# Eight-head layers: two rows half a trip apart, attention steps of one between feed-forward products of the other

## The reference

```python
def _layer(x, wqkv, qs, ksc, wo, lg, lb, w1, b1, w2, b2):
    h = shift_token(x)                 # second half of the features comes from the token before
    q, k, v = split(h @ wqkv)          # 8 heads of 64
    q = l2norm(q) * qs;  k = l2norm(k) * ksc
    q, k = rotary_xpos(q, k)
    o = local_attention(q, k, v)       # 4 windows of 128, each sees itself and the one before
    x = x + o @ wo
    h = layernorm(shift_token(x)) * lg + lb
    a, g = split(h @ w1 + b1)          # 682 columns each
    return x + (a * gelu(g)) @ w2 + b2
```

## Time and profile before

| | us |
|---|---|
| median of three runs | 2756.39 |
| profiled execution | 2757.84 |
| its span, first to last instruction | 2756.1 |
| first row transpose of the layers | 1282.3 |
| share of the layers | 1473.8 |

### The profile page before, as it was taken

One profiled execution on the slowest core, in us unless ns is written; L12 is line 12 of the kernel. 1 busy time (PEld: TensorE's weight loads), 2 busy tenths in 40 slices (PEclk: granted clock), 3 DMA queues, 4 the chain that ended last, 5 costly groups with the idle time before them and its releaser, 6 DMA issues.

```text
span 2756.1 us, 46420 instructions
## 1 busy us (share of the span) xinstructions
PE 2372.5 (86%) x16738; PEld 1794.1 (65%) x16738; DVE 1555.4 (56%) x4225; ACT 1207.0 (44%) x3055; POOL 933.5 (34%) x1360
## 2 busy tenths in 40 slices
PE   7999099996888888886789898898897988988988
PEld 4666099994455554545568676686676666766766
DVE  5564122224655656646757658658575586585754
ACT  1221033334555456562633725537336255373362
POOL 2221400004333343332723415326146253362442
PEclk9999599998797879897899999999999999999999
DMA  3221511112010110003000000000010100000000
GB/s 122 88 89 64 211 32 39 35 34 71 18 47 17 33 32 3 32 3 118 1 16 16 2 23 9 17 16 33 16 56 2 39 8 26 22 2 31 16 2 31
DMA packets 78000, 101.55 MB, mean 37 GB/s; under 512 B 6652, under 2 KB 70352, under 8 KB 77520
## 3 DMA queue, kind: packets, MB, share of 16 engines
q1 hardware_dynamic: 73184, 87.88, 9.5%
q0 software_dynamic: 3072, 8.39, 0.9%
q10 hardware_dynamic: 1520, 2.31, 0.2%
HBM read 62.51 MB, written 35.52 MB: 36 GB/s over the span
## 4 chain that ended last, share of the span: by engine, by line
PE 29%; DVE 14%; POOL 5%; issue 3%; ACT 2%; DVEq 0%; POOLq 0%; ACTq 0%
PE l_bank L1943 6%; PE l_bank L1944 5%; PE l_bank L1945 5%; PE l_bank L2050 4%; POOL l_probs L1588 3%; DVE l_work L1665 2%; DVE l_ss L1646 2%; PE l_turned L2003 2%; PE l_bank L1985 2%; PE l_bank L2019 2%; DVE l_probs L1663 1%; DVE l_probs L1684 1%; PE l_turned L1943 1%; PE l_turned L1945 1%; PE l_turned L1944 1%
## 5 line engine op out<-in xcount | busy, mean ns | idle before, releaser
L1024 DVE TENSOR_REDUCE c_cnmax<-cbank 128x1 f32<-128x384 f32 (+3 forms) x384 | 206.1, 596 | 107.4 <-PE cbank L1215 88.9
L1588 POOL TENSOR_SCALAR l_probs<-l_probs,l_rinv 128x256 f32<-128x256 f32 (+1 forms) x512 | 223.3, 454 | 127.5 <-DVE l_rinv L1689 126.4
L1862 ACT ACTIVATE l_probs<-l_probs,l_nmax 128x256 f32<-128x256 f32 (+1 forms) x512 | 239.4, 476 | 0.0
L1124 ACT ACTIVATE c_cprobsT<-cbank 128x384 f32<-128x384 f32 (+1 forms) x384 | 180.5, 522 | 97.5 <-PE cbank L1241 96.8
L1684 DVE CUSTOM_DVE_ANT_0 l_probs<-l_bank,mask 128x256 f32<-128x256 f32 (+1 forms) x512 | 169.1, 387 | 36.7 <-PE l_bank L1985 23.6
L1572 POOL TENSOR_TENSOR l_work<-l_work 128x512 f32<-128x512 f32 x64 | 82.7, 1292 | 272.8 <-DVE l_work L1665 271.8
L945 POOL TENSOR_SCALAR_AFFINE_SELECT c_cprobsT<-c_cprobsT 128x256 f32<-128x256 f32 x256 | 99.4, 411 | 165.9 <-ACT c_cprobsT L1124 163.8
L1985 PE MATMUL l_bank<-l_kT,l_flipped 64*128 64x256 f32 (+1 forms) x1024 | 152.4, 419 | 0.0
L1908 ACT ACTIVATE l_v<-l_bank,l_b 128x512 f32<-128x512 f32 (+1 forms) x96 | 66.1, 689 | 193.9 <-PE l_bank L1945 193.9
L684 PE MATMUL h_bank<-m_xsT,xn 128*128 128x128 f32 x1248 | 148.3, 278 | 0.3 <-DVE xn L621 0.3
L1943 PE MATMUL l_bank<-l_part,l_w_high 128*128 128x512 f32 (+1 forms) x288 | 123.5, 429 | 26.0 <-DVE l_yT L1755 26.0
(11 more groups left out here) (261 smaller groups left out, 6258.3 us busy)
## 6 DMA issues: line engine op xcount, KB each, us to landing
w<-in_W1T SPq DMA_DIRECT2D x8, 1024.0 KB, 7.9
w<-in_W2T SPq DMA_DIRECT2D x8, 1024.0 KB
l_came<-y_d SPq DMA_DIRECT2D x16, 512.0 KB, 4.2
xs_d<-zrow SPq DMA_DIRECT2D x8, 640.0 KB, 11.6
m_xs<-xs_d SPq DMA_DIRECT2D x39, 128.0 KB, 2.2
ys_d<-m_y SPq DMA_DIRECT2D x39, 128.0 KB, 1.7
c_came<-x_d SPq DMA_DIRECT2D x8, 512.0 KB, 4.6
y_d<-c_raw SPq DMA_DIRECT2D x8, 512.0 KB, 3.6
```

Source lines behind the costliest of these rows:

```text
L1024: dve.tensor_reduce(nmax[:, c % 2, qt, s, i:i + n], S, AX, ALU.max, negate=True).then_inc(nmax_ready[s], 1)
L1124: act.activation(probsT[s][:, c % 2, i, k0:k0 + w], turned_place(j, s)[:, 0:w], ACT.Exp).then_inc(probs_ready[s], 1)
L1588: pool.tensor_scalar(probs[s][:, held(u), h, 0:n], probs[s][:, held(u), h, 0:n], rinv[s][:, u, h:h + 1], 1.0, ALU.mult, ALU.mult)\
L1862: act.activation(probs[s][:, held(u), h, 0:n], probs[s][:, held(u), h, 0:n], ACT.Exp, bias=nmax[s][:, u, h:h + 1], scale=-1.0, accum_out=r ...
```

## The change

All of it is inside `phase_layers`. The work is cut into `HALVES` = 16 halves n; half n is one batch row in one layer (`place(n)`: row n mod 2 of trip n div 2). The program runs positions: while row n is in attention, row n - 1 is in its feed-forward. After the sixteenth half a seventeenth pass does only the feed-forward of the last row.

- A step is now one window and head pair of one row, in both 64-feature halves: 8 steps per half (`STEPS`), each with the same four scores, maxima, exponentials, scalings and transposes as a unit of before. There is one set of two score banks, one pair of `turned` banks, one `out` bank, and three banks for projections and hidden products (`free_bank`).
- `FLIP_LAG` goes from 3 to 2 and `OUT_LAG` from 4 to 3; `probs` has two buffers.
- The twelve hidden products of row n - 1 lie in positions 0 to 8 of the steps of row n (`HIDDEN_AT`), each in one of the three free banks, gate and a alternating.
- The gate products are copied out of PSUM by ScalarE and the a products by VectorE (`take_out`, six copies of 128 x 512 each per half, new). The Gelu of all six chunks runs later in SBUF in one batch, with its own table load at position 8; then `gated` with both operands in SBUF.
- The projection of row n + 1 runs alone, after the second product of row n - 1 and the transposes of row n.
- The reciprocals of the sums are one instruction per step for all four columns. Weight loads and splits of the second layer are spread over halves 7 to 9.

```diff
+        FLIP_LAG, OUT_LAG, SPAN = 2, 3, 11
+        HIDDEN_AT = ((0, 1), (2, 3), (4, 5), (6,), (7,), (8,), (9,), (10,), (11,), (), ())
...
+        probs = sb("probs", [P, 2, 2, 2, 2 * P])
+        probsT = sb("probsT", [P, 2, 2, 4, P])
...
             @block.vector
...
+                    for t in range(NT + 1):
+                        if t < NT:
+                            turn(t)
+                        if t == 0:
+                            between()
+                        if t:
+                            invert(t - 1)
+                        if t < NT:
+                            norms(t)
...
+                for n in range(HALVES + 1):
+                    att, ffn = n < HALVES, n > 0
+                    for p in range(SPAN):
+                        if att:
+                            if 0 <= p - FLIP_LAG < STEPS:
+                                pT_out(n, p - FLIP_LAG)
+                            if p < STEPS:
+                                row_max(n, p)
+                            if 0 < p <= STEPS:
+                                invert_sums(n, p - 1)
+                        if ffn:
+                            for k in HIDDEN_AT[p]:
+                                if k % 2:
+                                    take_out(n - 1, k)
...
+                        if ffn and p == 9:
+                            gated(n - 1, 0)
+                            gated(n - 1, 1)
+                    if att:
+                        residual(n, 0)
+                        residual(n, 1)
+                    if ffn:
+                        gated(n - 1, 2)
+                        low_units(n - 1, 0)
+                        gated(n - 1, 3)
+                        low_units(n - 1, 1)
+                    if att:
+                        residual(n, 2)
+                        residual(n, 3)
+                    if ffn:
+                        gated(n - 1, 4)
+                        low_units(n - 1, 2)
+                        gated(n - 1, 5)
+                        low_units(n - 1, 3)
+                    if n + 1 < HALVES:
+                        low_parts(n + 1)
+                    if ffn:
+                        low_units(n - 1, 4)
+                        low_units(n - 1, 5)
+                    if att:
+                        measure(n)
...
             @block.scalar
...
+                    for p in range(SPAN):
+                        if att:
+                            if 0 <= p - FLIP_LAG < STEPS:
+                                pT_out(n, p - FLIP_LAG)
+                            if p in (5, 7, 9):
+                                oT_out(n, (p - 5) // 2)
+                            if 0 < p <= STEPS:
+                                exps(n, p - 1)
+                        if ffn:
+                            for k in HIDDEN_AT[p]:
+                                if k % 2 == 0:
+                                    take_out(n - 1, k)
+                        if att and p < 2:
+                            qT_out(n, p + 2)
+                            kT_out(n, p + 2)
...
+                        if ffn and p == 8:
                             act.preload_act_table(ACT.Gelu)
+                            gelu(n - 1, 0)
...
             @block.tensor
...
+                def rotations(n):
+                    project(n, 0)
+                    project(n, 1)
+                    project(n, 2)
+                    flip_qk(n, 0)
+                    project(n, 3)
+                    flip_qk(n, 1)
...
+                    for p in range(SPAN):
+                        if att:
+                            if 0 <= p - FLIP_LAG < STEPS:
+                                flip(n, p - FLIP_LAG)
+                            if p < STEPS:
+                                scores(n, p)
+                            if 0 <= p - OUT_LAG < STEPS and p < SPAN - 1:
+                                output(n, p - OUT_LAG)
+                        if ffn:
+                            for k in HIDDEN_AT[p]:
+                                hidden(n - 1, k)
+                        if att:
+                            if p < 2:
+                                flip_qk(n, p + 2)
+                            if p == SPAN - 2:
+                                attended(n, 0)
+                                attended(n, 1)
+                            if p == SPAN - 1:
+                                output(n, p - OUT_LAG)
+                    if n + 1 < HALVES:
+                        flip_rows(n + 1)
+                    if att:
+                        attended(n, 2)
+                        attended(n, 3)
+                        shift(n)
+                    if ffn:
+                        contract(n - 1)
+                    if att:
+                        flip_hn(n)
+                    if n + 1 < HALVES:
+                        rotations(n + 1)
```

More of the change, by code:

```diff
@@ new lines, in _ @@
+                    if n:
+                        store(n - 1)
+                    if n == LAST + 1:
+                        load_w2(sp, 1)
+                    if layer:
+                        sp.wait_ge(hT_psum[s], pair * DC + DC)
+                        sp.dma_start(hn[s], g.x3_d[trip * NS + s].rearrange("(t p) n -> p t n", p=P)).then_inc(x_in[s], 16)
+                    if n == LAST:
+                        sp.wait_ge(affine[s], pair * DC + DC)
+                        load_ln(sp, 1)
@@ L1878, in _ @@
-                    for u in range(UNITS + OUT_LAG + 1):
-                        if 0 <= u - FLIP_LAG < UNITS:
-                            pT_out(u - FLIP_LAG)
-                        if u > OUT_LAG and (u - OUT_LAG) % 2 == 0:
-                            oT_out((u - OUT_LAG) // 2 - 1)
-                        for s in range(NS):
-                            if 0 < u <= UNITS:
-                                exps(s, u - 1)
-                        if u == UNITS:
-                            act.preload_act_table(ACT.Gelu)
@@ L1918, in _ @@
-                    if pair + 1 < TRIPS:
+                    for t in range(NT + 1):
+                        if t < NT:
+                            square(t, 0)
+                        if t:
+                            square_root(t - 1)
+                        if t < NT:
+                            square(t, 1)
+                            v_out(t)
+                        if 2 <= t < NT:
+                            qT_out(n, t - 2)
+                            kT_out(n, t - 2)
+                    act.preload_act_table(ACT.Exp)
@@ new lines, in exps @@
+                def exps(n, j):
+                    J = n * STEPS + j
+                    width = (1 + min(step_of(j)[1], 1)) * P
+                    for r in range(2):
+                        for h in range(2):
+                            act.wait_ge(nmax_ready, 4 * J + 2 * r + h + 1)
+                            a = probs[:, j % 2, r, h, 0:width]
+                            act.activation(a, a, ACT.Exp, bias=nmax[:, j, r, h:h + 1], scale=-1.0, accum_out=rsum[:, j, r, h:h + 1]).then_inc(probs_ready, 1)
@@ L2023, in hidden @@
-                    def hidden(s, c):
-                        if c >= 2:
-                            pe.wait_ge(u_done[s], pair * UC + c - 1)
-                        r = rows(c)
-                        for i in range(2):
-                            for k in range(DC):
-                                last = product(bank[s][2 * (c % 2) + i][0:r, :], [w1[a][:, k, i * HID + c * P:i * HID + c * P + r] for a in (1, 0)],
-                                               [a[:, k, 1:L + 1] for a in (part[s], yT[s])], k == 0, k == DC - 1)
-                        last.then_inc(ag_psum[s], 1)
@@ new lines, in attended @@
+                def attended(n, t):
+                    s, pair, layer, trip = place(n)
+                    pe.wait_ge(oT_ready, n * (STEPS // 2) + STEPS // 2 - 1 + t // 2)
+                    if t == 0:
+                        pe.wait_ge(wo_in, 16 * (layer + 1))
+                        pe.wait_ge(nmax_ready, 4 * STEPS * (n + 1))
+                    elif t >= 2:
+                        pe.wait_ge(y1_ready[s], pair * NT + t - 1)
+                    for c in range(HP2):
+                        last = pe.matmul(score_bank[t % 2][:, 0:D], oT[s][:, c, t * P:(t + 1) * P], wo[:, c, :], start=c == 0, stop=c == HP2 - 1)
+                    last.then_inc(wo_psum[s], 1)
@@ new lines, in contract @@
+                def contract(n):
+                    s, pair, layer, _ = place(n)
+                    pe.wait_ge(w2_split, 2 * (layer + 1))
+                    pe.wait_ge(u_ready[s], pair * UC + UC)
+                    for t in range(NT):
+                        if t >= 2:
+                            pe.wait_ge(y2_ready[s], pair * NT + t - 1)
+                        for c in range(UC):
+                            r = rows(c)
+                            last = product(turned_bank[t % 2][:, 0:D], [a[0:r, c, t * P:(t + 1) * P] for a in (u_high[s], u_low[s])],
```

(2 more changed lines are left out.)

988 lines of the change are left out of this document (507 added, 481 removed).

## The result

Median of four runs: 3037.9 us (3034.4 to 3042.0), against 2758.2 us (2755.2 to 2761.6, four runs) of the kernel before in the same session. The ratio is 1.101, with an interval of 1.099 to 1.103: 10% slower. The prediction had 2967 (2860 to 3110).

What follows compares the result with a forecast made beforehand. TensorE was nearest full; in the new steps the 5.7 us flip chain binds. Span 1284.6 + 92 + 14 x 103.2 + 101.2 + 44 = 2966.6, + 1.7 outside; profiled run 1.5 over median: 2967 us, range 2860 to 3110.

Steps and rivals of the forecast that it cites:

- Chain of 5.7 once per step: Steps: flip, copy, exponentials, reciprocal, GpSimd scaling, next flip take 5.7 us, once per step; positions 3 to 8 take 34.1.
- TensorE bound: Rival, chance 0.10 with faster: steps take TensorE's own 4.0 us, giving 2787, or 2645 without waits and clock term.
- Copies out of PSUM cost nothing: Steps: the twelve added copies, 0.7 us each, are hidden on VectorE and ScalarE; taken as nothing.
- Positions 0 to 2: Start of a half: scores(1) at 28.0 after a 3 us wait for row_max(0), flip(1) at 39.2 us.
- Tail: After the steps: output projections, shift, residuals, low parts end at 90.6 us; TensorE waits 4 before the second product.
- Second product: End of a half: second feed-forward product takes 10.0 us, bringing the next half at 100.7.
- clock term of 2.5: Per half: 2.5 us for slow clock after the two TensorE waits (3 and 4 us), making 103.2.
- No clock cost: Rival, chance 0.16: both waits too short to slow the clock, so the 2.5 us per half goes: 2930 us.
- Slow clock in the steps: Rival, chance 0.13: clock falls to 1.2 GHz in half the steps, 10 us more a half: 3110 us.
- the same chain of steps: 92: First half, no feed-forward beside it: same chain of steps, 92 us, with 2 for GpSimd's weight splits.
- Change of layer costs nothing: Change of layer: its 9 us now falls away, each load being issued over 20 us before use.
- Last pass: Last pass, only feed-forward: hidden products, Gelu batch, second product and end take 44 us.

Runs made afterwards that it cites:

- Kernels 1, 2 and 12: Changed kernel with FLIP_LAG 3, OUT_LAG 4: 2902.6 us; changed kernel with each step's reciprocal in two: 2945.5 us; best kernel with FLIP_LAG 2: 2883.7 us.
- kernel 3: Changed kernel with two of the three matmuls of each hidden product left out: 3045.1 us, ratio 1.104.
- kernel 4: Changed kernel with useless filler matmuls on TensorE, five ahead of scores(1) and seven ahead of the second product: 2990.3 us, ratio 1.084.
- best kernel: Changed kernel with FLIP_LAG 3, ScalarE's and VectorE's lists reordered, five filler matmuls ahead of scores(1), last pass chunk by chunk: 2701.7 us, ratio 0.982.
- kernel 11: The best kernel without its five filler matmuls ahead of scores(1): 2722.6 us, ratio 0.988.

## Why the prediction was right, and where it was off

The sign, the mechanism and the range held. The sum was 70 us of span short (3036.2 against 2966.6), and nearly all misses went the same way, so the total isn't right by misses that cancel. Of the signs named, the flips from 1 on were released by GpSimd and stood 5.15 to 6.1 apart (5.4 to 6.3 forecast); the two waits were 2.5 and 3.25 (3 and 4); TensorE was busy 81% of a steady half (near 80) and 74% between flips (60 to 70); a half took 105.9 (101 to 105). Step by step:

- *Chain of 5.7 once per step:* 5.6 measured. Positions 3 to 8 took 33.3, against 34.1 (flips at 41.8, 47.4, 53.0, 58.2, 63.4, 69.5 and 75.1 in the half from 1814.07). Kernels 1, 2 and 12 show that the chain is the cause, not only that it fits. The "TensorE bound" rival fell with kernel 3.
- *Copies out of PSUM cost nothing:* nothing contradicts it. GpSimd stays the releaser of the flips, no group of hidden products waits for a copy, and ScalarE and VectorE are idle before the chain's own copies in the steps. A kernel without the added copies wasn't tried.
- *Positions 0 to 2:* flip(1) at 41.8 instead of 39.2, + 2.6. Scores(1) came at 29.1 (28.0 forecast), behind a wait of 2.48 for row_max, and ran slow, 2.00 us instead of 1.11:

```profile
1843.13 2.00 PE L2120 MATMUL l_score<-l_kT,l_flipped 64*128 64x256 f32 x8 [2.48 <-DVE l_nmax L1753]
```

- *Tail:* from flip(7) to the second product 19.3, not 17.3, + 2.0. The attention output and output projection there run at a clock that I had not counted down (window), and the output stood waiting for oT_out, which the sum did not have at all (timeline):

```profile
1883.60:1903.40 19.80, 17.30 (x126) 13.28 (x126) 7.88 (x15) 12.33 (x25) 1.85 (x4) 0.83 0.00 1
```

```profile
1891.12 1.98 PE L2160 MATMUL l_out<-l_probsT,l_v 128*64 128x128 f32 x16 [1.27 <-ACT l_oT L1965]
1893.02 4.41 PE L2173 MATMUL l_score<-l_wo,l_oT 128*128 128x256 f32 x16
```

By the durations of before (1.09 and 3.72) the slow clock is 1.6 of this, the wait 1.3; from the last residual to the second product it was 0.7 shorter than the 5.6 of the sum.

- *Second product:* 11.4 instead of 10.0, + 1.4, also clock. These three misses are 6.0 together, less 0.8 of the steps; the clock term of 2.5 stood for them. So a half came out at 105.9 and not 103.2; over 15 halves that is 40 us of the 70. The mis-sized term is the clock's. Some 4.6 of the 6.0 are its: 1.6 behind scores(1) (with the clock held up there in kernel 4, flip(1) starts at 40.2 and not 41.8), 1.6 in the tail, 1.4 in the second product. I priced it by one wait of before, and there were three slow stretches: that is 2.1 a half too little, some 31 of the 40 us. The rest is scores(1), 1.1 late, and the wait of 1.3 for oT_out, less what the steps and the end of VectorE's list took less.
- *No clock cost:* this rival is refuted; kernel 4 gets 48 us back with the clock. The Trainium skill's page "TensorE: Matmul & The Clock Gate", section "Loop structure matters more than you think", has products stay fast where the other engines' work lies beside them; here that holds in the steps (0.95) and not at the seams between stages (0.76, 0.83, 0.86). By it the sum was 2930.
- *Slow clock in the steps:* wrong for the steady halves, right where no hidden products lie between: in the first half. The window of its steps:

```profile
1325.70:1358.00 32.30, 21.18 (x176) 16.01 (x176) 10.62 (x50) 13.10 (x47) 17.98 (x23) 0.50 0.00 1
```

The clock is at its lower level of 1.2 GHz throughout, flips take 1.12 instead of 0.72, and they stand 6.0 to 7.3 apart. The step of the prediction that failed is "the same chain of steps: 92": it took 102.2, + 10. From flip(1) to flip(7) it was 39.0 and not 34.1; 2.9 came ahead of that, where the clock was 0.52 from 1310.0 on, and 2.4 behind. Not all of it need be the clock: the longest distance, 7.3, holds a weight split of 5.96 us on GpSimd between two scalings, for which the sum had 2.
- *Change of layer costs nothing:* it cost 9.5 over three halves (108.9, 109.9 and 108.4). What failed is "each load is issued over 20 us before its use": the loads are early, but the weights must be split too, and GpSimd does it beside VectorE. In the second of the three halves (timeline):

```profile
2217.36 5.97 POOL L1633 TENSOR_TENSOR l_w_low<-l_w_raw,l_w_high 128x2728 fp32r<-128x2728 f32 x1
```

```profile
2218.14 0.42 DVE L1787 TENSOR_TENSOR l_y<-l_score,l_came 128x256 f32<-128x256 f32 x1 [1.30 <-PE l_score L2173]
2218.48 5.39 DVE L1774 SCALAR_TENSOR_TENSOR l_work<-l_work,l_b,l_flipped 128x512 f32<-128x512 f32 x1
```

The gating, 0.75 elsewhere, took 5.39 and ended 0.54 behind GpSimd's subtraction. GpSimd had been idle 5.21 ahead of its two instructions for these weights, until the load (issued at 2209.0) landed: the landing put the split beside the gating. The residuals behind it came late, and the shift waited 2.85 for them, so that the second product started 2.4 later than in other halves. That is 2.4 of the 4.0 extra of that half; the other 1.6 is the second product, which took 13.1 at 0.74 there. The 3.0 and 2.5 of its neighbours I did not follow up.
- *Last pass:* 47.6 against 44. The second product came at 31.9, 1.5 late, and ran slow: 11.7 in place of 10 (0.84 over the pass).

In sum: 10 for the first half, 40 for 15 halves (31 of them clock), 2 that the fifteenth did not save, 9.5 for the layer, 3.7 for the second half with its 109.6 us, and 3.6 for the last pass make 69; the misses are those 70 us.

## What to carry to other kernels

A chain that runs through several in-order engines sets a floor under a step's time: its length divided by the positions it may span. Write down the length (5.6 us here) before the lag is lowered to save a buffer: one position was worth 135 us, and 174 to 182 once the rest was mended. Then read each engine's list at the seams, for what a waiting consumer needs and what stands ahead of it: order alone gave 97 and 69 us, more than the fillers (48 and 20 us). And price a wait of TensorE with the slow stretch behind it.

## What the runs showed of the hardware

- *Work taken from TensorE can slow it.* 11.3 us of matmuls less a half lowered the mean granted clock of the span from 0.898 to 0.851 and gave no time (3045 against 3038); twelve useless matmuls more a half raised it to 0.912 and gave 48 us. In the best kernel five of them are worth 15 to 21 us.
- *The same steps ran at either level.* With hidden products between them and TensorE busy 24.6 of 33.3 us they were granted 0.95; with none between, in the first half, 0.50, although by the longer durations TensorE was busy 21.2 of 32.3 us.
- *VectorE is held by GpSimd only in some instructions.* In the rows above the residual, which reads one operand from PSUM and one from SBUF, took 0.42 beside GpSimd's long subtraction, as elsewhere; the gating, with two large operands in SBUF, was held for it. In kernel 11 a low part (`low_units`), also with two operands in SBUF and 0.68 elsewhere, took 6.43 beside the same subtraction of 6.26. The Trainium skill, page "SBUF — State Buffer", section "SBUF: two separate sides", says that VectorE and GpSimd share a pair of ports which one instruction takes whole, and names VectorE instructions with two SBUF inputs among those that need it: the trace agrees (0.42 and 5.39). So GpSimd's long splits belong beside copies out of PSUM, not beside gatings; no kernel here was built that way.
